# A node stage and its tables laid out with four consecutive nodes to a partition

## What is computed

```python
# layer 1: attention over incoming edges and a self loop, 4 heads of 64
x_proj = x @ lin_W.T
att    = leaky(s_src[src] + s_dst[dst] + e_att)       # 0.2 slope; the self loop has no edge term
alpha  = softmax of att over the edges of one dst
x      = layernorm(x + sum_over_edges(x_proj[src] * alpha) + bias)
# layer 2: a message network on both ends of every edge, mean over src
h      = tanh([x[src], x[dst]] @ W0 + b0)             # 512 -> 406
h      = tanh(h @ W1 + b1); h = h @ W2 + b2           # -> 323 -> 256
x      = layernorm(x + segment_mean(h * (e_embed @ Wg), src))
```

## Time and profile before

| | us |
|---|---|
| median of 3 runs | 4805.3 |
| lowest and highest | 4802.85, 4808.88 |
| span of the profiled execution | 4813.1 |

### The profile page before, as it was taken

How to read it: one execution, slowest core, us unless ns; L and a number is a source line. 1 busy time by engine, 2 the same in 40 slices (tenths; PEclk the granted TensorE clock), 3 DMA queues, 4 the chain that set the end, 5 groups by cost and what they waited for, 6 DMA issues and landing times. The chain is left out here.

```text
span 4813.1 us, 84225 instructions
## 1 busy us (share of the span) xinstructions
PE 3972.5 (83%) x23546; PEld 3291.7 (68%) x23546; DVE 3729.6 (77%) x11631; ACT 3089.0 (64%) x7157; POOL 2981.9 (62%) x2765
## 2 busy tenths in 40 slices
PE   5899999977777499999999799999999999999200
PEld 3466666655555399999999687777788778777200
DVE  6899999978888699898989476666666666666564
ACT  6866666645555266666666477776777767776575
POOL 1055556567777355555555377777777778777322
PEclk9999999988999699999999899999999999999655
DMA  4255554558666499999999577766767766766696
GB/s 105 51 171 169 168 171 167 169 148 212 199 201 202 151 360 364 349 365 353 365 359 362 175 152 154 153 149 153 152 150 153 154 152 149 153 150 152 218 394 261
DMA packets 717533, 1002.80 MB, mean 208 GB/s; under 512 B 186862, under 2 KB 591298, under 8 KB 704182
## 3 DMA queue, kind: packets, MB, share of 16 engines
q0 software_dynamic: 160768, 323.45, 30.3%
q10 hardware_dynamic: 245565, 375.01, 21.6%
q1 hardware_dynamic: 310861, 300.30, 19.8%
HBM read 567.01 MB, written 431.82 MB: 208 GB/s over the span
## 5 line engine op out<-in xcount | busy, mean ns | idle before, releaser
L1468 PE MATMUL bank<-w0r,n_x1T 128*128 128x406 f32 x4704 | 903.3, 351 | 41.1 <-ACT n_pa L1516 38.9
L1468 PEld LDWEIGHTS bank<-w0r,n_x1T 128*128 128x128 f32 x4704 | 868.0, 189 | 65.6 <-ACT n_pa L1516 63.4
L1612 POOL DMA_INDIRECT out_x<-u_sums,u_row x392 | 635.8, 1622 | 144.4 <-issue 117.1
L1664 PE MATMUL bank<-u_h,w1r 128*108 128x512 f32 (+1 forms) x2646 | 692.4, 407 | 0.0
L635 POOL DMA_INDIRECT DS<-payload,rank_int x392 | 378.2, 965 | 477.0 <-DVE rank_int L810 386.5
L1344 POOL DMA_INDIRECT n_cg<-CT,n_last x392 | 452.0, 1153 | 174.4 <-issue 95.2
L1664 PEld LDWEIGHTS bank<-u_h,w1r 128*108 128x108 f32 (+1 forms) x2646 | 444.5, 175 | 129.8
L1595 POOL DMA_INDIRECT u_pa<-PA,key_int x392 | 388.2, 990 | 167.2 <-issue 120.1
L891 POOL DMA_INDIRECT xg<-XP,ds x392 | 412.4, 1052 | 125.9 <-issue 121.3
L1664 PE MATMUL bank<-w2r,u_h 108*128 108x256 f32 x3528 | 479.2, 280 | 0.0
L427 PE MATMUL bank<-wst,xT 128*128 128x264 f32 x1568 | 421.3, 391 | 51.0 <-DVE xps L436 50.8
(11 more groups left out here) (319 smaller groups left out, 10080.4 us busy)
## 6 DMA issues: line engine op xcount, KB each, us to landing
PA<-n_pa ACTq DMA_DIRECT2D x98, 816.0 KB
PB<-n_pb ACTq DMA_DIRECT2D x98, 812.0 KB
XP<-xps ACTq DMA_DIRECT2D x98, 528.0 KB
CT<-ct ACTq DMA_DIRECT2D x98, 528.0 KB
n_xp<-XP SPq DMA_DIRECT2D x98, 528.0 KB
xin<-in_x SPq DMA_DIRECT2D x97, 512.0 KB
n_x<-in_x SPq DMA_DIRECT2D x97, 512.0 KB, 9.8
out_x<-n_x ACTq DMA_DIRECT2D x97, 512.0 KB, 5.0
```

Source lines behind the costliest of these rows:

```text
L1468: o = nc.tensor.matmul(acc, xT[s][p][:, k, e], w0r[q][:, 2 * half + k, :], start=(n == 0), stop=(n == len(terms) - 1))
L1612: pool.indirect_dma_start(out=out, out_offset=bass.IndirectOffsetOnAxis(ap=si[s][:, j:j + 1], axis=0), in_=yo[s][:, j, :], in_offset=None, ...
L1664: o = nc.tensor.matmul(acc, a[p], b[q], start=(start and n == 0), stop=(stop and n == 2))
```

## The change

The digits of src are taken like those of dst, so that both counts and both results stand in quad order. `lastd` is then written directly in the histogram stage, and the 16 selection matrices, the 16 products with them, a copy and a semaphore step go. In the node stage every load and store goes by `nodes` where it went by `tiles`: XP, x, out, PA and PB. The list `il` of the gathers has the same order, so gather j now takes the last edges of the nodes 4p + j. The arithmetic of the node stage is the same. The tables in memory have the same rows in the same places.

```diff
-                    c.did(nc.vector.tensor_scalar(ki[1][:], KI[:, 1, 0:NT], P - 1, None, ALU.bitwise_and))
-                    c.did(nc.vector.tensor_scalar(ki[3][:], KI[:, 1, 0:NT], 7, None, ALU.arith_shift_right))
+                    c.did(nc.vector.tensor_scalar(ki[1][:], KI[:, 1, 0:NT], 2, P - 1, ALU.arith_shift_right,
+                                                  ALU.bitwise_and))
+                    c.did(nc.vector.tensor_scalar(ki[3][:], KI[:, 1, 0:NT], 9, 2, ALU.arith_shift_right,
+                                                  ALU.logical_shift_left))
+                    c.did(nc.vector.tensor_scalar(ki[5][:], KI[:, 1, 0:NT], G - 1, None, ALU.bitwise_and))
...
-                    c.did(nc.vector.tensor_scalar(HI[1][:], ki[3][:], -0.5, None, ALU.add))
+                    c.did(nc.vector.scalar_tensor_tensor(HI[1][:], ki[3][:], -0.5, ki[5][:], ALU.add, ALU.add))
...
-                        nc.gpsimd.memset(place[:], 0.0).then_inc(h_pad, 1)
-                        pool.wait_ge(h_pad, 9)
-                        for r in range(G):
-                            for k in range(G):
-                                nc.gpsimd.affine_select(out=place[:, r * G + k, :], in_=place[:, r * G + k, :],
-                                                        compare_op=ALU.not_equal, fill=1.0, base=k - r * P,
-                                                        pattern=[[-1, P]], channel_multiplier=G).then_inc(h_pad, 1)
...
-                        c.did(nc.vector.tensor_scalar(lastf[:], tot[1][:], float(NP), None, ALU.add))
+                        c.did(nc.vector.tensor_scalar(lastd[:], tot[1][:], float(NP), None, ALU.add))
...
-                        pe.wait_ge(r_ot, GROUPS)
-                        pe.wait_ge(h_pad, 9 + G * G)
-                        by_quad = lastf[:].rearrange("p (g t) -> p g t", t=G)
-                        by_tile = LB[:, 0:NT].rearrange("p (g t) -> p g t", t=G)
-                        for r in range(G):
-                            for k in range(G):
-                                o = nc.tensor.matmul(by_tile[:, :, r], place[:, r * G + k, :], by_quad[:, :, k],
-                                                     start=(k == 0), stop=(k == G - 1))
-                        o.then_inc(r_tk, 1)
+                        pe.wait_ge(h_pad, 8)
...
                         dve.wait_ge(r_tk, 2)
-                        nc.vector.tensor_copy(lastd[:], LB[:, 0:NT])
-                        dve.wait_ge(r_tk, 3)
...
-                        sp.dma_start(xpn[s][:], tiles(XP, g)).then_inc(n_ld[s], 16)
-                        load_rows(sp, xin[s], x, g, last, n_x[s])
+                        sp.dma_start(xpn[s][:], nodes(XP, g)).then_inc(n_ld[s], 16)
+                        load_nodes(sp, xin[s], x, g, last, n_x[s])
...
-                            act.dma_start(tiles(out, g), x1[s][:]).then_inc(x1_st[s], 16)
+                            act.dma_start(nodes(out, g), x1[s][:]).then_inc(x1_st[s], 16)
...
-                        act.dma_start(tiles(PA, g), pa[s][:]).then_inc(pa_st[s], 16)
-                        act.dma_start(tiles(PB, g), pb[s][:]).then_inc(pb_st[s], 16)
+                        act.dma_start(nodes(PA, g), pa[s][:]).then_inc(pa_st[s], 16)
+                        act.dma_start(nodes(PB, g), pb[s][:]).then_inc(pb_st[s], 16)
```

More of the change, by code:

```diff
@@ L215, in gnn_kernel @@
         krf = [alloc(srt, f"key_rowsf{q}", [P, NC, P]) for q in range(2)]
-        ki = [alloc(srt, f"key_digit{q}", [P, NT], i32) for q in range(5)]
+        ki = [alloc(srt, f"key_digit{q}", [P, NT], i32) for q in range(6)]
         h_pad, h_loaded, h_rows, h_psum, h_chain = (sem("h_pad"), sem("h_loaded"), sem("h_rows"), sem("h_psum"),
@@ L221, in gnn_kernel @@
         KEYS = 16 * (2 * len(loads) + 2)
-        KEYS_READY = 13
+        KEYS_READY = 14
         ph = ExitStack()
@@ L371, in gnn_kernel @@
             PD = alloc(srt, "payload", [P, NT, 8])
-            lastf = alloc(srt, "last_by_quad", [P, NT])
-            place = alloc(srt, "place", [P, G * G, P])
             steps = alloc(srt, "step_difference", [P, P])
@@ L603, in gnn_kernel @@
                 OT, UB, XO = B[3][:, 0:G * P // 2].bitcast(f16), (B[4], B[5]), (B[2], B[7])
-                LB = B[3]
                 prior = alloc(ph, "prior", [P, G * P])
@@ L903, in _ @@
                         c.did(nc.vector.memset(ks[s][:], 0.0))
-                    dve.wait_ge(h_pad, 10 + G * G)
+                    dve.wait_ge(h_pad, 9)
                     c.did(nc.vector.tensor_scalar(pk[0][:], pn[:], 2, G - 1, ALU.arith_shift_right, ALU.bitwise_and))
@@ L1390, in row @@
                                                           ALU.mult))
-                        dve.wait_ge(n_x[s], 16 * (i + 1) + 16 * last)
+                        dve.wait_ge(n_x[s], 16 * (i + 1))
                         cr.wait()
@@ L1496, in norm @@
                         if not last:
-                            act.dma_start(tiles(out, g), x1[s][:]).then_inc(x1_st[s], 16)
+                            act.dma_start(nodes(out, g), x1[s][:]).then_inc(x1_st[s], 16)
                             return
-                        act.dma_start(tiles(out, g, TAIL_TILES), x1[s][:, 0:TAIL_TILES, :]).then_inc(x1_st[s], 16)
-                        act.dma_start(out[N - TAIL_ROWS:N, :], x1[s][0:TAIL_ROWS, TAIL_TILES, :]).then_inc(x1_st[s], 16)
+                        act.dma_start(out[(GROUPS - 1) * G * P:N, :].rearrange("(p t) w -> p t w", t=G),
+                                      x1[s][0:TAIL_QUADS]).then_inc(x1_st[s], 16)
                     def high(g, s):
@@ L1540, in _ @@
                         tables(GROUPS - 2 + s, s)
-                    act.wait_ge(x1_st[0], 16 * PAIRS)
-                    act.wait_ge(x1_st[1], 16 * PAIRS + 16)
                     for s in range(2):
+                        act.wait_ge(x1_st[s], 16 * PAIRS)
                         act.wait_ge(pa_st[s], 16 * PAIRS)
```

## The result

The kernel after takes 4834.9 us (median of 5 runs, 4828.6 to 4852.7) where the one before took 4805.3 beside it (4802.0 to 4818.8): a ratio of 1.0061, 95% interval 1.0041 to 1.0080. It is 0.6% slower. The forecast was 4779 with a range up to 4806. The sign was wrong, and what happened is in essence the rival with a chance of 0.15, priced at 4842.

A forecast was written before the change was run, and what follows sets the result against it. The prediction took the node stage to be TensorE plus the wait for a gather. Gains of 23 (node stage), 1 (long stalls), 1 (stage ends) and 0.5 (rank stage), 26 us, took 4805.3 to 4779, range 4757 to 4806.

The forecast's parts named there:

- the rival with a chance of 0.15: Node stage, slower: the fourth gather lands behind PA's 816 KB, 2.2 us later; 37 us more, 4842; chance 0.15.
- The margin of 0.11 us: Node stage: in a group without a wait, the fourth gather's issue ended 0.11 us before the PA store's.
- the alternation: Node stage: a group that waits gives its successor more room, so a microsecond of landing is worth half of period.
- Less DMA work per group: Node stage: longer runs, stores at 25 and loads at 21.5 GB/s per engine, 8.6 us instead of 9.4, 0.8 less.
- How much reaches the fourth gather: Node stage: of the saved DMA work, 0.7 us shortens the fourth gather's landing, between nothing and 1.2.
- The forecast of 23 to 35 us: Node stage gain: 0.24 us per group over 97 periods, 23 us; without any wait at most 35 us.
- The three long stalls: Node stage: three waits, 16.8 us together, from POOL standing still 2.1 us; they stay, together 1 us cheaper.
- Rank stage: Without the 16 selection products VectorE ends earlier, but POOL's last scatter must land; gain 0 to 1 us, taken 0.5.
- TensorE's floor: Node stage: TensorE's own need per group, 9.02 us of products and 1.04 of transposes, 10.06 us.
- the signs listed for a wrong forecast: Node stage: unchanged share and landing (rate), 2 us waits behind PA (order), or unchanged period without waits (cover).

The follow-up runs named there:

- shift5_before: Kernel before, with a one-word ScalarE copy and a wait for its end ahead of the PA store; 4803.2 us, ratio 0.9997.
- shift5_after: Kernel after, with a one-word ScalarE copy and a wait for its end ahead of the PA store; 4805.9 us, ratio 1.0008.
- early_after: Kernel after, with POOL copying the list of rows before the power, so the gathers are issued about 1 us earlier; 4753.6 us, ratio 0.9894.
- guard_after: Kernel after, with ScalarE posting PA only when POOL has issued the fourth gather and run a memset behind it; 4808.9 us, ratio 1.0009.
- pad_after: Kernel after, with 8 unused words behind each SBUF row of x, XP, x1, PA and PB, so every run is one row; 4842.7 us, ratio 1.0072.
- shift_after: Kernel after, with a one-word ScalarE copy ahead of the PA store and no wait for its end; 4837.0 us, ratio 1.0066.
- stores_before: Kernel before, with only ScalarE's three stores (out, PA, PB) by nodes, values not the program's; 4838.0 us, ratio 1.0065.
- late2_before: Kernel before, with a POOL memset of 192 words ahead of the fourth gather of each group; 5017.5 us, ratio 1.0452.

## Why the prediction was wrong

**The step that failed** is in the rivals: "Against it: both posts hang on the same VectorE instructions, and the margin was positive each time except where POOL stood still." The margin of 0.11 us was read correctly in one pair, and the groups that waited had 0.08 in the median and 0.02 at least. But it was not positive each time: at 1669 us, where POOL had not stood still, it was -0.32, and that group of the kernel before shows what a turned order costs (2.25 us of wait). The margin was then treated as fixed by a common releaser. But one of its ends was the end of an instruction that the change itself rewrites. "Bytes, instructions and waits on the engines stay as they were; ... So only the DMA engines' time per byte can move" was the sentence too much: the duration of a posting instruction moved from 0.378 to 0.338 us, twice between the normalization and PA's end. The row with 0.38 for PA stood in the earlier trace rows, and the trace of before had the other one as well. ScalarE's store of the last norm goes in one run per partition; durations in ns, kernel before:

```profile
L2023 ACTq DMA_DIRECT2D out_x<-f_y x34: 338/338/345, 4560.0 to 4734.3; - x34
```

2 x (0.378 - 0.338) = 0.08 us against a margin of 0.08: both numbers stood in the trace of the kernel before, and they put the flip near even odds, not at 0.15. The trigger given for the rival ("ScalarE comes to its PA store earlier" because the waits go) was not the one that acted.

**The size of that rival** was near: 37 us and 4842 against 41 us in the stage and 4834.9. It had 2.2 us per flipped group at one in three, 0.73 per group; it is 1.75 at one in two, 0.88. That the two come near each other is partly luck, since the share of groups and the price were off in opposite directions. One in two follows from the alternation told with the earlier trace rows: a group that waits gives the next one room, whose margin is then +1.3.

**Less DMA work per group**: right. Stores were put at 25 and came to 23.8, loads at 21.5 and came to 24.75, together (2.19 / 23.8 + 1.07 / 24.75) in ms per GB over 16 engines, 8.45 us against the 8.6 forecast.

**How much reaches the fourth gather**: the term of 0.7 us was wrong where it was applied. It started from the 4.76 us of one pair of groups, and the median of the groups that waited was 4.18. With the order intact the gather lands 4.1 to 4.25 us after its start in either layout (`shift5_before`, `shift5_after`), close to the least of 3.6 of any gather; there was no 0.7 to take. The bound "at least nothing, if its landing is fixed delay" was nearer. The same saved work is worth 0.32 us of period, 31.5 us, once the gathers are issued a microsecond earlier, when they land 5.4 us after their start in the old layout and 4.2 in the new. The forecast of 23 to 35 us fits a kernel that has that lead, and this one has not.

**The three long stalls** were forecast to stay. POOL stands 2.13 us three times in the kernel after too, 28 groups apart, an even number, and so each time on the same side of the alternation, ahead of a group with room. VectorE then waits 0.24 to 0.71 us, and 16.8 us are gone. In `shift5_after`, without the strict alternation, they are back. This hides part of the loss: the ordinary waits rose from 30.3 to 76.8 us.

**Rank stage**: 0.5 forecast, about 1.5 seen. From the start of the last scatter to the next stage's first POOL instruction it was 4.10 us and is 2.64. First before, then after:

```profile
1022.22 0.13 POOL L879 IOTA m_partition<- 128x1 int32 x1 [3.12 <-POOLq L618]
```

```profile
1017.64 0.99 POOL L633 DMA_INDIRECT DS<-r_s_dst,head_rows  x1 [0.30 <-issue]
1020.28 0.13 POOL L862 IOTA m_partition<- 128x1 int32 x1 [1.65 <-POOLq L611]
```

Before, the end of the stage hung on the counts (VectorE's reciprocals end at 1021.87), not on the scatter's landing as assumed. It does not show in the total: the first power of the node stage comes anywhere from 1626 to 1648 us in these runs.

**TensorE's floor** of 10.06 us was right, since `early_after` runs at 10.09. Of the signs listed for a wrong forecast, "DMA share falls, yet waits of some 2 us appear where a fourth gather was issued after PA" is what the profile shows, except that the flip is by the ends of two posts and not by their starts.

What stays open: why a gather posted 0.62 us ahead of PA landed 7.8 and 8.0 us after its start in two groups of `guard_after`; why waits of a microsecond stand in `pad_after` at margins of up to 1.7; how much of the 8 us at a margin of -1 is PA and PB and how much the loads; and whether the end of the posting instruction is the moment that counts, or one that lies at a fixed distance from it. That its sign decides is shown on both sides of zero in the new layout over the whole stage, and in the old one on the positive side over the whole stage and on the negative side, close to zero, in four groups.

## What to carry to other kernels

Where two engines post DMAs within a few tenths of a microsecond of each other and one of them is waited for, treat their order as a result to be computed from every instruction between the last common releaser and the two ends, the posting instructions included, and ask of each edit whether it touches one of them. A margin of 0.1 us is no margin: here a lead of a microsecond for the small urgent transfer, put in beside the cheaper large one, turned a loss of 0.6% into a gain of 1.1%. An edit that is meant to move a post is read first in the timeline, since a pause can vanish in an idle gap or be passed by the queue.

## What the runs showed of the hardware

- **Place in the queues.** A gather whose post ended 0.02 to 0.06 us behind that of an 816 KB store landed 5.6 us after its start in the kernel after (5.4 in `shift_after`, 5.5 in `stores_before`); 0.01 to 0.14 ahead of it, 4.1 to 4.2; 1 us behind, with PB's post and the starts of two loads ahead as well, 8.0.
- **The second of two close posts is held back.** The store's first packet started 0.71 us after its post where that ended just ahead of the gather's, and 1.53 to 1.57 where it ended just behind, with packets of 1.6 KB and of 6.5 KB.
- **Posting time depends on the shape.** 0.338 us for 128 runs (PA by `nodes`), 0.378 for 512 runs (by `tiles`), 0.55 for 512 padded runs.
- **A POOL gather whose post begins in the middle of a 128x1024 VectorE operation ends it 0.90 to 0.93 us after the start of VectorE's next instruction** (69 of 69 in the kernel before); begun outside of these operations it took 0.94 to 1.07 (184 gathers). Of 77 gathers in the kernel before that took over 1.2 us, 68 ended 0.88 to 0.96 us after the start of a VectorE instruction, and all 66 of `late2_before`. A start 0.10 us into such an operation instead of just ahead of it cost 1.01.
- **POOL stands at fixed places.** It stood 2.13 us ahead of its gathers number 114, 226 and 338 of the stage, 112 apart, in both kernels; why is not shown.
- **A post does not wait for the ScalarE instruction ahead of it.** It started 0.15 us into copies of 0.19 and 0.41 us.
- **Rates.** Runs of 4 to 6.5 KB went at 23.8 GB/s per engine for stores and 24.75 for loads, against 22.1 and 20.9 for 1 to 1.6 KB. `early_after` moved 376 GB/s in this stage.
